# A bias moved from a matmul to VectorE, with the order of five engines' work rewritten around it

## What is computed

```
mod = silu(c) @ wmod                      # 16 x 6 x 128
h = layernorm(x) * (1 + ca) + sa
Q, K, V = h@Wq + bq, h@Wk + bk, h@Wv + bv # 16 heads of 8
Q, K = elu(Q) + 1, elu(K) + 1
a = linear attention of Q, K, V, divided by Q . sum(K)
x1 = layernorm(h + a@Wo + bo) * g1 + beta1
y  = relu(x1@W1 + b1) @ W2 + b2           # hidden width 512
x = x + ga * (layernorm(x1 + y) * g2 + beta2)
h = layernorm(x) * (1 + cb) + sb
r = sigmoid(mix_r(h) @ W_r);  k = relu(mix_k(h) @ W_k)^2
out = x + gb * r * (k @ W_v)              # mix_r, mix_k: weighted sums of a token and the one before it
```

## Time and profile before

| what | us |
|---|---|
| median of 3 runs | 163.59 |
| profiled execution, its own time | 162.81 |
| its span | 160.7 |
| TensorE busy | 155.6 (97%) |
| ScalarE busy | 127.3 (79%) |
| VectorE busy | 123.1 (77%) |
| GpSimd busy | 104.6 (65%) |

### The profile page before, as it was taken

The page is one execution under the profiler, slowest core; times in us unless marked ns, Lnnn a source line. Parts: engine busy times, 40 slices in busy tenths (PEclk is TensorE's granted clock), DMA queues, the critical chain, the costliest instruction groups (busy, mean ns, idle before and its releaser), DMA issues.

```text
span 160.7 us, 4111 instructions
## 1 busy us (share of the span) xinstructions
PE 155.6 (97%) x1151; PEld 145.1 (90%) x1151; DVE 123.1 (77%) x572; ACT 127.3 (79%) x346; POOL 104.6 (65%) x243
## 2 busy tenths in 40 slices
PE   7899999999999999999999999999999999999992
PEld 6778998999999999999999999999999999888891
DVE  3766878597887969696978779796969777888842
ACT  4256777889797979898997979797989989656562
POOL 4337567576676767787676767676877755973631
PEclk9999999999999999999999999999999999999999
DMA  4926299920010101010100101010101001010112
GB/s 122 269 90 174 67 276 369 423 115 0 2 37 0 33 0 33 4 37 0 34 5 0 33 4 35 0 35 4 33 0 35 4 0 33 2 37 0 35 33 67
DMA packets 8974, 9.94 MB, mean 62 GB/s; under 512 B 724, under 2 KB 7416, under 8 KB 8952
## 3 DMA queue, kind: packets, MB, share of 16 engines
q1 hardware_dynamic: 8656, 9.60, 18.8%
q10 hardware_dynamic: 296, 0.08, 0.2%
HBM read 7.55 MB, written 2.13 MB: 60 GB/s over the span
## 4 chain that ended last, share of the span: by engine, by line
PE 93%; DMA 2%; DVE 2%; ACT 1%; issue 0%; SPq 0%; DVEq 0%
PE bank L1266 16%; PE bank L1156 16%; PE bank L1145 8%; PE bank L1238 5%; PE bank L1194 5%; PE bank L1150 5%; PE bank L1222 4%; PE bank L1182 4%; PE bank L1230 4%; PE bank L1378 4%; PE bank L1210 4%; PE bank L1206 4%; PE bank L1249 3%; DMA kqvo<-in_kqvo 2%; PE bank L1219 1%; PE bank L1398 1%
## 5 line engine op out<-in xcount | busy, mean ns | idle before, releaser
L1156 PE MATMUL bank<-w,hid 128*128 128x128 f32 x240 | 31.7, 275 | 0.0
L1266 PE MATMUL bank<-x1T,w 128*128 128x256 f32 x120 | 30.9, 381 | 0.0
L1156 PEld LDWEIGHTS bank<-w,hid 128*128 128x128 f32 x240 | 29.3, 192 | 0.0
L347 ACT ACTIVATE hid<-bank,b_cols 128x256 f32<-128x256 f32 x60 | 26.0, 511 | 1.1 <-PE bank L1266 1.1
L544 POOL TENSOR_TENSOR rstd_n<-vare_n,power 128x2 f32<-128x2 f32 x30 | 23.8, 792 | 2.4
L1266 PEld LDWEIGHTS bank<-x1T,w 128*128 128x128 f32 x120 | 21.5, 190 | 2.7 <-DVE z L803 0.2
L710 DVE TENSOR_SCALAR ny<-bank,mv_ny,rstd_ny 128x128 f32<-128x128 f32 x32 | 11.7, 406 | 9.0 <-POOL rstd_ny L544 9.0
L323 ACT ACTIVATE hT<-bank,modT 128x256 f32<-128x256 f32 x16 | 9.0, 565 | 11.3 <-PE bank L1145 11.3
L540 POOL TENSOR_TENSOR vare_n<-mv_n,eps 128x2 f32<-128x2 f32 x30 | 5.9, 195 | 17.2 <-DVE mv_n L704 17.1
L292 ACT ACTIVATE n<-x_all,shift_n,rstd_n 128x128 f32<-128x128 f32 x27 | 11.8, 485 | 2.5 <-POOL shift_n L552 2.5
L317 ACT ACTIVATE keepT<-bank,modT 128x255 f32<-128x255 f32 x26 | 13.1, 555 | 0.0
(11 more groups left out here) (187 smaller groups left out, 454.7 us busy)
## 6 DMA issues: line engine op xcount, KB each, us to landing
gm_rows<-mod_rows_dram SPq DMA_DIRECT2D x2, 960.0 KB, 9.5
out<-out_sb SPq DMA_DIRECT2D x15, 128.0 KB, 1.8
gm_rows<-mod_rows_dram SPq DMA_DIRECT2D x1, 768.0 KB, 6.7
w<-in_w SPq DMA_DIRECT2D x1, 512.0 KB, 5.6
x_all<-in_x SPq DMA_DIRECT2D x1, 512.0 KB, 5.6
bv_row<-bv_rows_dram SPq DMA_DIRECT2D x1, 512.0 KB, 7.1
bv_row<-bv_rows_dram SPq DMA_DIRECT2D x1, 384.0 KB, 4.4
gm_rows<-mod_rows_dram SPq DMA_DIRECT2D x1, 384.0 KB, 3.7
```

What stands on the lines that cost most here:

```text
L347: last = nc.scalar.activation(hid[:, f, :], bank[:, f % 2 * L:(f % 2 + 1) * L], ACT.Relu, bias=b1_cols[:, f:f + 1])
L1156: last = nc.tensor.matmul(banks[6][:, c * D:(c + 1) * D], hid[:, f, c * 128:(c + 1) * 128], w2[:, f, :], start=False, stop=(f == FF - 1 an ...
L1266: return nc.tensor.matmul(bank[:, f % 2 * L:(f % 2 + 1) * L], w1[:, f * 128:(f + 1) * 128], x1T[:, :], start=True, stop=True)
```

## The change

The bfloat16 matmul of the key bias goes. The bias is built once as `bias_rows` (128 x 128, negated on ScalarE from bank 6), put into bank 4 by an identity matmul for sample 0, and for samples 1 to 15 added by VectorE in a new instruction, `k_biased`, which writes `kb`. `k_exponent` and `k_elu` read `kb`. The receptance product waits for `kb` where it waited for `k_sb`.

```diff
@@ TensorE, k_product
-                need(pe, k_ok, s)
-                nc.tensor.matmul(chunked(banks[4]), ones3[:, :], bias_parts...broadcast_to([128, NC, D]),
-                                 start=True, stop=False)
+                need(pe, kb_ok, s - 1)
@@ VectorE
+            def k_biased(s):
+                need(dve, k_mm, s + 1)
+                need(dve, bias_rows_ok, 1)
+                nc.vector.tensor_tensor(kb[:, :, :], chunked(banks[4]), bias_rows...broadcast_to([128, NC, D]),
+                                        ALU.add).then_inc(kb_ok, 1)
@@ ScalarE, k_exponent
+                need(act, kb_ok, s)
+                source = kb[:, :, :] if s else chunked(banks[4])
@@ ScalarE, step
-                hidden_out(sd, 0)
-                attention_turned(sb_)
+                if draining(t):
+                    hidden_out(sd, 0)
+                    attention_turned(sb_)
+                else:
+                    attention_turned(sb_)
+                    hidden_out(sd, 0)
@@ GpSimd, step: the scale of n1 two samples ahead (rstd_n1 and shift_n1 are now two tiles each)
-                if live(t + 1):
-                    first_scale(sa + 1)
+                if t == 3:
+                    first_scale(4)
...
+                if live(t + 2):
+                    first_scale(sa + 2)
@@ TensorE, step
-                    n1_transposes(sa)
...
+                feed_forward_out(2, FF).then_inc(z_mm, 1)
+                if live(t + 1):
+                    n1_transposes(sa + 1)
+                if live(t - 4):
+                    value_of_mix(sc)
@@ the start, TensorE
-            keep_warm(2)
...
-            keep_warm(WARM_N1)
...
-                pe.wait_ge(n1_half, 1)
-                n1_transposes(0)
-                direct_row(0)
+                pe.wait_ge(n1_turn, 1)
+                transpose_in(banks[0], n1[1], hT_mm)
...
-                second_modulation((2, 5), 2)
                 n1_transposes(1)
+                second_modulation((2, 5), 2)
...
-                feed_forward_out(2, FF).then_inc(z_mm, 1)
+                feed_forward_out(2, 3)
+                n1_transposes(3)
+                feed_forward_out(3, FF).then_inc(z_mm, 1)
@@ the start, VectorE (bias_part, four instructions on the bias's parts, goes)
                 x_stats(2)
                 denominators(0)
-                x_mv(2)
                 reciprocals(0)
+                k_biased(1)
                 attention(0)
+                x_mv(2)
                 k_elu(1)
+                direct_weights(1)
@@ the tail, ScalarE
+            h2_of_last(1)
             act.wait_ge(r_mm, s14 + 1)
             act.wait_ge(prod_ok, s14)
             nc.scalar.activation(tanh_r...).then_inc(tanh_ok, 1)
-            h2_of_last(1)
             squared_relu_of_last(0)
+            squared_relu_of_last(1)
             tanh_of_last(0)
-            squared_relu_of_last(1)
             tanh_of_last(1)
@@ the tail, TensorE
             value_product(s14)
+            key_last(1)
             receptance_last(0)
-            key_last(1)
             value_last(0)
```

More of the change, by code:

```diff
@@ L290, in take_n1 @@
                 wait_x(act, s)
-                for c in chunks:
-                    last = nc.scalar.activation(n1[s % 2][:, c, :], x_all[:, NC * s + c, :], ACT.Identity,
-                                                scale=rstd["n1"][:, c:c + 1], bias=shift_n1[:, c:c + 1])
+                for c in range(NC):
+                    last = n1_part(s, c)
                 last.then_inc(n1_ok, 1)
-            take_n1(0, (0,))
+            act.wait_ge(bias_mm, 1)
+            act.wait_ge(const_pool, 1)
+            nc.scalar.activation(bias_rows[:, :], banks[6][:, D:2 * D], ACT.Identity, scale=-1.0,
+                                 bias=one_pair[:, 0:1]).then_inc(bias_rows_ok, 1)
+            act.wait_ge(x_in[0], 16)
+            act.wait_ge(shift_n1_ok, 1)
+            n1_part(0, 0)
             act.wait_ge(cols_ok, 2)
@@ L360, in first_steps @@
             def first_steps():
-                h_turned(0)
+                act.wait_ge(hT_mm, 1)
+                nc.scalar.activation(hT[0][:, :], banks[0][:, 0:L], ACT.Identity, scale=mod_col(CA, 0),
+                                     bias=shift_first[:, :]).then_inc(hT_ok, 1)
+                n1_part(0, 1).then_inc(n1_ok, 1)
                 k_exponent(0)
@@ L977, in step @@
[L977 to L990 removed]
+                y_norm(sb_)
+                gated(sc)
@@ L1386, in step, with value_of_mix @@
                     feed_forward_out(3, FF).then_inc(z_mm, 1)
-                else:
-                    feed_forward_out(2, FF).then_inc(z_mm, 1)
+                    return
+                if t == 3:
+                    feed_forward_out(0, 2)
+                    value_of_state(sa)
+                    need(pe, hidb_ok, sd + 1)
+                else:
+                    value_of_state(sa)
+                    feed_forward_out(0, 2)
+                feed_forward_out(2, FF).then_inc(z_mm, 1)
+                if live(t + 1):
+                    n1_transposes(sa + 1)
+                if live(t - 4):
+                    value_of_mix(sc)
+            def value_of_mix(s):
+                need(pe, ksq_ok, s + 1)
+                need(pe, wvg_ok, s + 1)
+                need(pe, q_ok, s + 5)
+                need(pe, prod_ok, s)
+                for c in range(NC):
+                    last = nc.tensor.matmul(banks[5][:, c * D:(c + 1) * D], ksqT[:, c * 128:(c + 1) * 128], gate_tile(s)[:, :],
+                                            start=True, stop=True)
+                last.then_inc(v_mm, 1)
             steps(step)
```

277 lines of the change are left out of this document (126 added, 151 removed).

## The result

| kernel | median us | executions | ratio to before, 95% interval |
|---|---|---|---|
| before | 163.17 | 4 | |
| after | 160.86 | 4 (160.80 to 161.23) | 0.986 [0.982, 0.991] |

The change is worth about 1.4% in this comparison, 2.3 us. The forecast was 162.1 us with a range from 161.1 to 163.4, so the time lies 0.24 us under the range. The profiled execution took 160.80 us, with a span of 159.1: the span fell by 1.6 us, where the sum of the prediction said 1.5. The mechanism was nearly right and the time was not; both need an explanation.

The account below looks back on a forecast made before the run. TensorE's work was taken to bound the full steps, waits the two ends. Steps 1.32, start 0 and tail 0.19 sum to 1.5 us off the 163.59 median: 162.1 us, range 161.1 to 163.4.

Parts of the forecast that it names:

- Full steps, 1.32 us: Samples 4 to 15: twelve bias matmuls taken out of TensorE's chain at 0.11 us each give 1.32 us.
- `kb`, 0.42 us, hidden: VectorE's new bias addition takes 0.42 us a step and ends 0.3 us before `exp_k`, so it is hidden.
- `k_sb`, from 2.9 to 3.35 after the attention product: In each full step VectorE's `k_sb` ends at 3.35 us, with 0.4 us left before the state product at 3.75.
- rival 3: Key path across three engines becomes the bound at the state product, if 0.6 us late: slower, 165.7 us; chance 0.07.
- `exp_k` from SBUF, no difference: ScalarE's `exp_k` reading SBUF instead of a bank takes no longer, judged by rows of 416 and 410 ns.
- ScalarE's `n`, 0.3 to 0.4 us of room: In full steps ScalarE's `n` still ends 0.3 to 0.4 us before its transpositions, now due at 8.0 us.
- The start, sum 0: Start: 0.56 us early gain is spent by sample 2's late `mv_n`, TensorE recovers the loss; sum 0, give or take 0.4.
- The tail, 0.19: Last half's key ahead of receptance and its square ahead of `tanh`: `out_last` 0.19 us sooner, bounds 0 and 0.25.
- The sum, 1.5: Whole kernel: full steps 1.32, start 0 and tail 0.19 together give a gain of 1.5 us.
- 163.59 - 1.5 = 162.1 for the median.: Whole kernel: median before of 163.59 less the gain of 1.5 gives 162.1 us; 161.3 for an execution like the profiled one.
- the chance of 0.44: Whole kernel: chance 0.44 of being faster by over 1%, that is below 161.95 us.
- The removed warm-up matmuls I give no case: Start: removing TensorE's warm-up matmuls has no effect, as the clock is full from the first slice and gaps grow no longer.

## Why the prediction missed, step by step

- **Full steps, 1.32 us.** Size right: from sample 4's attention product (before 41.13, after 41.07) to sample 14's (128.97, 127.77) 1.15 us in ten steps, and 1.27 in all when a matmul is put back. The reason was half right. "Only work taken away, not reordering, shortens them" holds as far as it goes: the new order with a matmul in the old place gives 8.77. But taking away was not enough either. In the old order the removal gives nothing, because the condition "as long as the other engines still deliver in time" fails at `hT` and at the attention's copy. The chain had no piece called a wait because the bias matmul stood in its time. The prediction asks of neither whether it is in time, and does not mention ScalarE's new order, which is worth 0.14 a step. That the change held both reorderings made the 1.32 come true, and for the prediction that was luck.
- **`kb`, 0.42 us, hidden.** It took 0.37, and was out 0.36 us before `exp_k`. Right that it is hidden.
- **`k_sb`, from 2.9 to 3.35 after the attention product.** It ran from 2.91 to 3.61. With two inputs from SBUF it met GpSimd's `wv_gate`, which before lay elsewhere (71.61 us); its mean rose from 419 to 615 ns. I had used this very effect for sample 2's `rstd_n` and not here. That left of the room of 0.4 us at the state product a wait of 0.01 to 0.02 a step: the place that rival 3 names was reached, its cost was not.
- **`exp_k` from SBUF, no difference.** Its mean went from 475 to 507 ns. By the Trainium skill (VectorE: DVE Perf Modes, the section on the TRN2 errata) 43 were to be expected; the measured 32 are nearer to it than to the 6 ns of the pair of rows I went by, which are of two different functions. Behind it `k_sb` starts 0.04 later (2.91 against 2.88 after the attention product), and no more than the state product's 0.01 to 0.02 a step can come of that.
- **ScalarE's `n`, 0.3 to 0.4 us of room.** No wait at its transpositions in any settled step.
- **The start, sum 0.** `mv_n` at 12.97, `vare_n` at 13.30 (13.3 forecast), sample 1's attention product at 16.43 (16.5 to 16.7), 0.16 gained at 32 us. The sum was right and the loss at sample 1 a little smaller than forecast, and the experiment with `mv_n` forward shows the cause. The contention that I put on `rstd_n` (0.2) fell on `vare_n` instead: 0.42 beside `k_sb`, 0.20 in the kernel where it runs before it. The Trainium skill names contention of GpSimd with VectorE's instructions with two SBUF inputs (GPSIMD Engine Reference, Specifications), and the rows agree. But lying beside one another is not enough for it, as the last section shows, and the prediction's "against about 0.70 otherwise" passes over that.
- **The tail, 0.19.** 0.27 by the profiles, from both sides (0.27 undone, 0.30 alone), a little over the upper bound of 0.25. The mechanism is as described.
- **The sum, 1.5.** The span fell by 1.6, of which 1.3 come from the steps and 0.27 from the tail. Right.
- **"163.59 - 1.5 = 162.1 for the median."** This step failed. I had computed 161.3 for an execution like the profiled one, and 160.80 came; 0.1 of the rest is the span, 0.4 the time around it (2.1 to 1.7), which I took as the same for both kernels. Then I carried the 0.8 us by which the three runs shown lay above the profiled one over to the changed kernel, as if it were part of the kernel's work. It was not: the median of 61 more executions is 162.77, next to the profiled 162.81, and what lifts single executions (the start's clock and the time behind the span) is smaller or absent in the changed kernel. The 0.8, 0.4 and 0.1, less the 0.06 by which the median of after lies over its profiled execution, are the miss of 1.24 us. The prediction knew that the median before was "known to no better than its runs (162.75 to 163.77)", used this for the chance of 0.44, and left it out of the range: its lower end of 161.1 stands on the median of 163.59 as well. Against 162.77 the change gives 1.9 us.
- **"The removed warm-up matmuls I give no case: the clock is full from the first slice."** Wrong reading of a right row: the distances of the matmuls showed the lower level until 4.6 us in that very profile (0.213 against 0.111).

What stays open: how much of the two high runs shown first was the start and how much the time around the span, and why the changed kernel is spared the latter. That it is less exposed to a late start is read from its relatives; of itself there are four executions.

## What to carry to other kernels

A chain that names only one engine does not prove that its instructions are the bound: compare the length of each link with its like, since an instruction that can be removed may be standing in the time of a wait, and then only removal together with the reordering pays. Take the sum against the profiled execution and carry that through; the distance between a median of three and the profile belongs to the executions, and whether a changed kernel keeps it is a term of its own. Where a queue of small instructions feeds another engine (`mv_n`), its place in the queue is worth more than the length of anything in it: 0.56 us for an instruction of 0.25.

## What the runs showed of the hardware

- TensorE's first rise to the higher clock level came anywhere from 4.0 to 7.4 us in kernels that had done the same until 3.6, and the row of the granted clock reads full before it; the distance of two like matmuls (0.213 or 0.111) is the witness.
- The clock fell from the higher level after TensorE had started nothing for 1.8 us in one profile, and stayed low for 3.4 us (granted 0.50). Sample 0's attention product came 1.8 us later than in the other profile of that kernel (13.22 against 11.47).
- A piece of instructions of 16 KB loaded behind the last instruction goes with 0.1 to 0.6 us more of time outside the span, and one profile has such extra time without it.
- VectorE and GpSimd slow one another when both read two SBUF tiles, but never the instruction that is already running. GpSimd's `vare_n`, started 0.06 us behind `k_sb`, took 0.42 us instead of 0.20, and `k_sb` its usual 0.43. `k_sb`, started 0.04 behind `wv_gate`, took 0.70 instead of 0.42, and `wv_gate` its usual 0.46. In the kernel before, where `k_sb` reads a bank, it took 0.42 beside `wv_gate` too. `rstd_n`, started 0.02 behind `qT`, took 0.93; started ahead of it, it is not slowed, and neither is `qT`. In the kernel before:

```profile
20.55 0.69 POOL L544 TENSOR_TENSOR rstd_n<-vare_n,power 128x2 f32<-128x2 f32 x1
...
20.84 0.39 DVE L848 SCALAR_TENSOR_TENSOR qT<-exp_q,relu_q 128x256 f32<-128x256 f32 x1
```

Over the fourteen profiles `rstd_n` took 0.90 to 0.96 us in each of the 139 places where it starts 0.01 to 0.06 behind `qT`, and 0.69 to 0.70 where it starts ahead of it and nothing else of this kind runs. By these rows, starting a little earlier or later than the other is worth 0.2 us. Why the order decides is not shown.
